# FFN pairs of a transformer layer: mixing the channels behind the third product, sums of x taken from PSUM, gates all 144 wide, weights in another order

## The chip, the cores and the metric

The kernel runs on one core of a Trainium2 chip. A core has TensorE (PE, whose weight loads are shown apart as PEld), VectorE (DVE), ScalarE (ACT), GpSimd (POOL) and SyncE (SP, which here only issues DMAs). All tensors of the computation are 32-bit floats. The metric is the device time of one execution in microseconds; lower is better.

## The reference

The layer takes x of 32 x 64 x 1024 and does two things in turn: a long convolution with attention on top, added to x, and then the FFN, added again. The change is in the FFN and in the weights and loads around its start:

```python
def _moe_lora(xf, gate_W, A, B):
    gate_probs = jax.nn.softmax(xf @ gate_W.T, axis=-1)
    weights, sel = jax.lax.top_k(gate_probs, TOP_K)          
    weights = weights / jnp.sum(weights, axis=-1, keepdims=True)
    w_dense = jnp.zeros((T, E), xf.dtype).at[jnp.arange(T)[:, None], sel].add(weights)
    h = jnp.einsum('td,erd->ter', xf, A)
    h = h * (w_dense[:, :, None] * SCALING)
    return jnp.einsum('ter,eor->to', h, B)
...
out = xf @ W_base.T + _moe_lora(xf, gate_W, A, B)
...
x = x + attention(convolution(x, ...), ...)
x = x + ffn(mix(x, weights, condition), ...)
```

`mix` multiplies the 64 positions of each of the 32 sequences by one of 16 matrices of 64 x 64, which the sequence's condition picks. What comes out is the FFN's input.

## The kernel before

The 2048 tokens are 16 tiles of 128, and two tiles are a pair: the FFN has `NP` = 8 pairs. Each engine runs its own program, written out by hand in order; semaphores with counts (`pe_p`, `v_xs`, `a_xfhi` and so on) tie them together.

A pair's product with W_base, 256 tokens x 1024 x 1024, is done as a Strassen-Winograd scheme: seven products (`product`, idx 0 to 6) of 128 x 512 x 512 instead of eight. Their left operands are four blocks of the mixed x (A11, A12, A22 and A21) and sums of them, S1 to S4. Each operand is kept as a high part in a format with a short mantissa and a low part that is the rest, and a product makes three passes (high by high, high by low, low by high), so it is 12 matmuls with 128x512 outputs. The right operands, combinations of W_base, are 14 units of weights (`w4_*`, two to a product). They are fetched by SP (`load_w4`), turned into a high part by ScalarE (`w4_hi`) and a low part by VectorE or, for units 7, 9, 11 and 13, by GpSimd (`w4_lo`).

For one pair PE does in order (`ffn_matmuls`): product 0, the gates and ranks (`gates_and_ranks`, 32 matmuls into PSUM bank 0), products 1, 2 and 3, two transposes of the weighted h (`turn_h`), product 4, six matmuls with the expert weights (`experts`), the channel mix of the next pair's two tiles (`mix_channels`, 128 small matmuls in the trace, into PSUM banks 0 to 3), product 5, two more expert matmuls, product 6. `added` makes PE wait until VectorE has taken a bank.

From the mixed x in PSUM, ScalarE copies the four blocks out (`x_hi`, into xs) and makes seven high parts from them (xf). VectorE forms the sums (`combine_x`) and the low parts of A11, A12 and A22 (`x_lo`), GpSimd the low parts of the sums (`combined_lo`). The gates of the next pair need the parts of A11, A12, S1 and A22. VectorE adds every finished bank into x1 (`add_to`), and picks the experts (`gate_choice`, `gate_weights_of_tokens`). SP stores x1 tiles when they are done and fetches those of the pair after next (`ffn_transfers`, `load_x1`, a ring of four tiles).

Ahead of pair 0, SP's queue (`attention_transfers`) holds, in order: x1 tiles 0 and 1, the gate weights, the store of x1 tile 14, a wait for the last projection but one, units 8 to 13 of the weights, the store of tile 15, the expert weights in two halves, x1 tiles 2 and 3. ScalarE's program for the FFN (`ffn_hi`) begins with a wait for the expert weights (`ld_p4`), VectorE's (`ffn_sums`) with the low part of weight unit 8.

## Time and profile before

| what | value |
|---|---|
| median of 3 runs | 909.04 us (907.42 to 910.8) |
| the profiled execution's own time | 911.1 us |
| its span, first to last instruction | 909.3 us |
| PE matmul busy | 876.0 us, 96% of the span |
| PE weight loads busy | 732.9 us, 81% |
| VectorE busy | 500.3 us, 55% |
| GpSimd busy | 465.9 us, 51% |
| ScalarE busy | 233.0 us, 26% |
| mean granted TensorE clock | 0.987 of full speed |

The busy share of PE is no measure of how near it is to its peak, since matmuls are pipelined and overlap in the records: what counts is the distance from one start to the next. All times of the profile are microseconds from the span's start. A granted clock of 1.00 is 2.4 GHz, 0.50 is 1.2 GHz. A row of the timeline merges neighbours of one kind: "x4" are four instructions, and the time is from the first's start to the last's end. What stands in square brackets is how long the engine was idle before the row, and who released it.

### The profile page before, as it was taken

How to read it: one execution, taken by the hardware profiler on the slowest of the kernel's cores; microseconds unless marked ns; L12 is line 12 of the kernel's file. 1: busy time of each engine (PE TensorE's matmuls, PEld its weight loads, DVE VectorE, ACT ScalarE, POOL GpSimd, SP SyncE). 2: the span in 40 equal slices, each digit the busy share in tenths (PEclk: the TensorE clock that was granted, in tenths of full speed). 3: DMA queues.
4: the chain of work that ended last, by engine and by line, in shares of the span. 5: the costliest groups of instructions: out<-in, count | busy, mean ns of one | idle time of the engine just before them, and what ended most of it. 6: DMA issues, size and time to landing. Idle time of an engine off the chain costs nothing.

```text
span 909.3 us, 24331 instructions
## 1 busy us (share of the span) xinstructions
PE 876.0 (96%) x10726; PEld 732.9 (81%) x10726; DVE 500.3 (55%) x880; ACT 233.0 (26%) x401; POOL 465.9 (51%) x346
## 2 busy tenths in 40 slices
PE   3999999999999999999999999999978999999998
PEld 3889999988888888887777777777766888888887
DVE  7465551123432222278887778888357666635663
ACT  4454542000000000032232223334233122211220
POOL 3444564103295557679878888877363233303330
PEclk9999999999999999999999999999998999988999
DMA  3789877315444322274444455553360221022201
GB/s 101 180 208 216 197 200 199 134 46 185 174 128 108 77 70 70 58 247 119 131 145 149 149 194 175 165 176 118 130 231 1 93 94 58 37 93 93 88 24 76
DMA packets 94554, 116.86 MB, mean 129 GB/s; under 512 B 44017, under 2 KB 58353, under 8 KB 94449
## 3 DMA queue, kind: packets, MB, share of 16 engines
q1 hardware_dynamic: 91456, 114.27, 42.3%
q8 instruction: 85, 1.39, 0.6%
q10 hardware_dynamic: 2480, 0.51, 0.3%
q0 software_dynamic: 512, 0.53, 0.2%
q14 instruction: 21, 0.16, 0.1%
HBM read 81.42 MB, written 33.85 MB: 127 GB/s over the span
## 4 chain that ended last, share of the span: by engine, by line
PE 83%; DVE 8%; DMA 2%; issue 2%; ACT 2%; SPq 1%; POOL 1%; DVEq 0%; POOLq 0%
PE ps L972 24%; PE ps L1250 19%; PE ps L1552 10%; PE ps L635 9%; PE ps L936 5%; PE ps L646 4%; PE ps L1206 3%; PE ps L1186 3%; DVE xf L1518 3%; PE ps L1568 2%; PE ps L1468 2%; ACT xs L1505 1%; PE ps L1570 1%; DMA toep<-kpad 1%; SPq L592 1%
## 5 line engine op out<-in xcount | busy, mean ns | idle before, releaser
L1552 PE MATMUL ps<-wb_hi,xf 128*128 128x512 f32 x448 | 153.3, 413 | 5.9 <-DVE x L1695 5.9
L1518 POOL TENSOR_TENSOR xf<-xs,xf 128x512 fp32r<-128x512 f32 x32 | 54.8, 1741 | 148.7 <-ACT xf L1511 148.7
L972 PE MATMUL ps<-y_hi,w_hi 128*128 128x512 f32 x320 | 125.3, 391 | 0.0
L972 PE MATMUL ps<-y_hi,w_lo 128*128 128x512 f32 x320 | 124.7, 390 | 0.0
L972 PE MATMUL ps<-y_lo,w_hi 128*128 128x512 f32 x320 | 124.7, 390 | 0.0
L1552 PEld LDWEIGHTS ps<-wb_hi,xf 128*128 128x128 f32 x448 | 88.5, 198 | 26.9 <-DVE x L1695 6.6
L1250 PE MATMUL ps<-y_hi 128*128 128x512 f32 x256 | 103.1, 403 | 0.2 <-issue 0.2
L635 PE MATMUL ps<-xc,toep 64*128 64x192 f32 (+4 forms) x1088 | 96.9, 330 | 3.5 <-DMA toep<-kpad 1.8
L1250 PE MATMUL ps<-y_hi,y_lo 128*128 128x512 f32 x256 | 100.2, 391 | 0.0
L1250 PE MATMUL ps<-y_lo,y_hi 128*128 128x512 f32 x256 | 100.2, 391 | 0.0
L635 PEld LDWEIGHTS ps<-xc,toep 64*128 64x128 f32 x1088 | 91.2, 187 | 6.6 <-issue 4.5
L1552 PE MATMUL ps<-wb_lo,xf 128*128 128x512 f32 x224 | 91.1, 406 | 0.0
L1084 POOL TENSOR_TENSOR rot<-rot,cst 128x512 f32<-128x512 f32 x40 | 53.7, 1343 | 58.1 <-DVE rot L1054 58.0
L1278 POOL TENSOR_TENSOR sc<-sc,stat 128x1024 f32<-128x1024 f32 x32 | 60.9, 1905 | 38.4 <-DVE stat L1274 38.4
L1054 DVE LOAD_MASK_SELECT rot<-ps x40 | 0.6, 14 | 134.1 <-PE ps L972 118.5
L972 PEld LDWEIGHTS ps<-y_hi,w_hi 128*128 128x128 f32 x320 | 60.1, 188 | 12.6
L972 PEld LDWEIGHTS ps<-y_hi,w_lo 128*128 128x128 f32 x320 | 60.1, 188 | 12.6
L972 PEld LDWEIGHTS ps<-y_lo,w_hi 128*128 128x128 f32 x320 | 60.1, 188 | 12.3
L1292 POOL TENSOR_TENSOR sc<-sc,stat 128x1024 f32<-128x1024 f32 x32 | 67.8, 2119 | 2.2 <-DVE stat L1288 2.2
L769 POOL TENSOR_TENSOR y_lo<-ym,y_hi 128x256 fp32r<-128x256 f32 x32 | 30.3, 948 | 70.2 <-ACT y_hi L758 70.0
L1088 POOL TENSOR_TENSOR rf<-rot,rc 128x512 f32<-128x512 f32 x40 | 52.8, 1320 | 17.8 <-DMA k_rows<-rf 14.8
L1695 DVE TENSOR_TENSOR x<-ps,x 128x512 f32<-128x512 f32 x64 | 42.1, 685 | 35.2 <-PE ps L1552 29.6
(183 smaller groups left out, 1596.4 us busy)
## 6 DMA issues: line engine op xcount, KB each, us to landing
toep<-kpad SPq DMA_DIRECT2D x124, 136.0 KB
xc<-in_dram SPq DMA_DIRECT2D x32, 256.0 KB, 4.5
q_rows<-rf SPq DMA_DIRECT2D x32, 256.0 KB, 2.6
q<-q_rows SPq DMA_DIRECT2D x16, 512.0 KB, 3.9
xr<-in_dram SPq DMA_DIRECT2D x16, 512.0 KB, 4.7
x_scratch<-xr SPq DMA_DIRECT2D x16, 512.0 KB, 3.0
x<-x_scratch SPq DMA_DIRECT2D x16, 512.0 KB, 4.3
out_dram<-x SPq DMA_DIRECT2D x15, 512.0 KB, 3.4
```

Of the source, the lines that this page charges most:

```text
L635: mm = pe.matmul(ps[:, 2 * (n % 3) + r, d * NB:NJ * NB], toep[rows, n % TR, at:at + P], xc[rows, n // XH % XR, 1 - c, n % XH, 0:(NJ - d) * ...
L646: mm = pe.matmul(ps[half * HALF:(half + 1) * HALF, 2 * (n % 3) + r, d * NB:NJ * NB], toep[rows, n % TR, at:at + HALF], xc[rows, n // XH % ...
L936: mm = pe.matmul(out, wv[a][:, j, h * P:(h + 1) * P], y[b][:, j, b0:b1, s0:s1], start=(j == 0 and a + b == 0), stop=(j == NJ - 1 and a == 1))
L972: mm = pe.matmul(kq_bank(n), w[a][:, j, :], yt[b][:, j, g * 512:(g + 1) * 512], start=(j == 0 and a + b == 0), stop=(j == NJ - 1 and a == 1))
L1084: gp.tensor_tensor(r, r, across(C("sin"), 8), ALU.mult).then_inc(g_rsin, 1)
L1088: gp.tensor_tensor(rf[:, (NVB + n) % SR, :], rot[:, n % RR, :], rc[:, n % RR, :], ALU.add).then_inc(g_rsum, 1)
L1250: mm = pe.matmul(ps[:, 6 + n, :], heads, wo(c, t)[:, n, :], start=(at == 0), stop=(at == 3 * NQT - 1))
L1278: gp.tensor_tensor(sc_groups(u), sc_groups(u), along(stat[:, u % CR, 0, :], S), ALU.subtract).then_inc(g_sub, 1)
L1292: gp.tensor_tensor(sc_groups(u), sc_groups(u), along(stat[:, u % CR, 2, :], S), ALU.mult).then_inc(g_prob, 1)
L1518: return eng.tensor_tensor(xf(i, op, 1)[:], xs(i, op), xf(i, op, 0)[:].bitcast(F32), ALU.subtract)
L1552: mm = pe.matmul(dst, xf(i, idx, a)[:, t, :], wb(c, idx, t), start=(start and t == 0 and a + c == 0), stop=(t == 3 and a == 1), skip_group ...
L1695: v.tensor_tensor(x, src, x, ALU.add).then_inc(v_sum_out, 1)
```

## The change

It is all in the FFN and the loads around its start.

- The channel mix of the next pair is moved from behind the expert matmuls to behind product 2, with a wait until VectorE has summed the gates' bank 0.
- The turned h goes to the sum bank that the pair doesn't use (bank 7 or 4), no longer to bank 1, into which the mix writes. The wait for the last projection's copy (`a_pr`) moves ahead of the first turn for that.
- ScalarE copies only A21 out of PSUM; the high parts of A22, A11 and A12 are made straight from PSUM (`x_of_mixed`), the high parts of the sums behind the turned h (`x_of_sums`): 8 operations a pair instead of 11.
- VectorE's sums and low parts take one operand from PSUM. They are seven as before, in two groups, `combine_first` ahead of the low part of h and `combine_last` behind it. `combined_lo` is `sums_lo` now, with the same four operations on GpSimd.
- The 16 gate matmuls of a pair whose left operand is a low part become 144 columns wide, as the other 16 are, instead of 72.
- SP fetches x1 tiles 2 and 3 before the weights, and units 12 and 13 behind the expert weights. ScalarE waits for the expert weights behind the gates' exponential of pair 0. VectorE takes the first add of pair 0 ahead of the low part of unit 8, and units 10, 12 and 13 change places with work on x.

```diff
 def attention_transfers(sp):
...
             sp.dma_start(wg_raw[:, :, 1, :], w_ffn[:, :, 0:NPROJ]).then_inc(ld_wg, 16)
+            load_x1(sp, 2)
             store_x1(sp, NPAIR - 2)
+            load_x1(sp, 3)
             sp.wait_ge(pe_y, 2 * NPAIR - 1)
-            for u in range(8, 14):
+            for u in range(8, 12):
                 load_w4(sp, u)
             store_x1(sp, NPAIR - 1)
...
-            load_x1(sp, 2)
-            load_x1(sp, 3)
+            load_w4(sp, 12)
+            load_w4(sp, 13)
...
+        def mixed_lo(v, i, op):
+            hi_made(v, i, op)
+            v.tensor_tensor(by_batch(xf(i, op, 1)[:]), mixed(*MIXED[op]), by_batch(xf(i, op, 0)[:]).bitcast(F32),
+                            ALU.subtract).then_inc(v_xflo, 1)
...
+        def combine_first(v, i):
+
+            hi_made(v, i, A22)
+            v.wait_ge(a_x21, i + 1)
+            v.tensor_tensor(by_batch(xs(i, S1)), mixed(1, 1), by_batch(xs(i, S3)), ALU.add).then_inc(v_xs, 1)
+            mixed_lo(v, i, A22)
+            hi_made(v, i, A12)
+            v.wait_ge(v_xs, 4 * i + 1)
+            v.tensor_tensor(by_batch(xs(i, S3)), mixed(0, 0), by_batch(xs(i, S3)), ALU.subtract).then_inc(v_xs, 1)
+            v.tensor_tensor(by_batch(xs(i, S2)), by_batch(xs(i, S1)), mixed(0, 0), ALU.subtract).then_inc(v_xs, 1)
+
+        def combine_last(v, i):
+            v.wait_ge(v_xs, 4 * i + 3)
+            v.tensor_tensor(by_batch(xs(i, S4)), mixed(0, 1), by_batch(xs(i, S2)), ALU.subtract).then_inc(v_xs, 1)
+            mixed_lo(v, i, A11)
+            mixed_lo(v, i, A12)
...
 def gates_and_ranks(pe, i):
...
-                        pe.matmul(gate_bank[:, k, :], xf(i, op, 0)[:, t, :], w[:, first + t, :, :].rearrange("p a n -> p (a n)"),
-                                  start=(op in (A11, S1) and t == 0), stop=False)
-                        mm = pe.matmul(gate_bank[:, k, 0:NPROJ], xf(i, op, 1)[:, t, :], w[:, first + t, 0, :],
-                                       start=False, stop=(op in (A12, A22) and t == 3))
+                        for part in range(2):
+                            mm = pe.matmul(gate_bank[:, k, :], xf(i, op, part)[:, t, :], w[:, first + t, :, :].rearrange("p a n -> p (a n)"),
+                                           start=(op in (A11, S1) and t + part == 0), stop=(op in (A12, A22) and t + part == 4))
...
 def ffn_matmuls(pe):
...
                 product(pe, i, 2, sum_bank(i))
+                if i + 1 < NP:
+                    pe.wait_ge(v_gate, GATE_STEPS * i + 1)
+                    mix_channels(pe, 2 * i + 2)
+                    mix_channels(pe, 2 * i + 3)
                 added(pe, 8 * i + 2)
                 product(pe, i, 3, D_BANK)
+                if i == 0:
+                    pe.wait_ge(a_pr, 2 * NPAIR)
                 turn_h(pe, i)
...
 def ffn_hi(act):
-            act.wait_ge(ld_p4, 16 * 2)
...
                 if i == 0:
+                    act.wait_ge(ld_p4, 16 * 2)
                     act.activation(bexp_hi[:], bexp_raw[:], ACT.Copy).then_inc(a_p4, 1)
-                    for u in range(10, 14):
-                        w4_hi(act, u)
+                    w4_hi(act, 10)
+                    w4_hi(act, 11)
+                if i + 1 < NP:
+                    x_of_mixed(act, i + 1)
                 act.wait_ge(pe_ht, i + 1)
...
 def ffn_sums(v):
-            w4_lo(v, 8)
             for i in range(NP):
                 v.wait_ge(pe_p, 7 * i + 1)
                 add_to(v, i, 0, 0, sum_bank(i))
+                if i == 0:
+                    w4_lo(v, 8)
                 gate_choice(v, i)
```

How the programs of the engines stand before and after, at three places. PE in pair 0, around the mix of tiles 2 and 3 (x1_2, x1_3; wb_hi_9 is the high part of weight unit 9, xf_0_4_1 the low part of operand 4), before:

```order
L1552 MATMUL ps<-wb_hi_9,xf_0_4_1 128x512
L1584 MATMUL ps<-bexp_hi,ht 128x512
L1585 MATMUL ps<-bexp_lo,ht 128x512
L1584 MATMUL ps<-bexp_hi,ht 128x512
L1585 MATMUL ps<-bexp_lo,ht 128x512
L1584 MATMUL ps<-bexp_hi,ht 128x512
L1585 MATMUL ps<-bexp_lo,ht 128x512
L1468 MATMUL ps<-craw,x1_2 64x64 x32
L1468 MATMUL ps<-craw,x1_3 64x64 x32
L1552 MATMUL ps<-wb_hi_10,xf_0_5_0 128x512
```

And after, the same mix of the same pair:

```order
L1561 MATMUL ps<-wb_hi_5,xf_0_2_0 128x512
L1561 MATMUL ps<-wb_lo_5,xf_0_2_0 128x512
L1561 MATMUL ps<-wb_hi_5,xf_0_2_1 128x512
L1471 MATMUL ps<-craw,x1_2 64x64 x32
L1471 MATMUL ps<-craw,x1_3 64x64 x32
L1561 MATMUL ps<-wb_hi_6,xf_0_3_0 128x512
```

The mix stood between the expert matmuls and product 5 (unit 10), and stands between products 2 (unit 5) and 3 (unit 6).

VectorE in pair 0, from the last part of the gate steps (hw is the weighted h, ht its low part), before:

```order
L1688 TENSOR_TENSOR hw<-gsum,gt 128x2x64 x2
L1695 TENSOR_TENSOR x1_0<-ps,x1_0 128x512
L1412 TENSOR_TENSOR wb_lo_10<-wb_raw_10,wb_hi_10 128x1024
L1412 TENSOR_TENSOR wb_lo_12<-wb_raw_12,wb_hi_12 128x1024
L1717 TENSOR_TENSOR ht<-ps,ht 64x256
L1695 TENSOR_TENSOR x1_1<-ps,x1_1 128x512 x2
L1488 TENSOR_TENSOR xs_1_1<-xs_1_6,xs_1_4 128x512
L1491 TENSOR_TENSOR xs_1_4<-xs_1_0,xs_1_4 128x512
```

After:

```order
L1705 TENSOR_TENSOR hw<-gsum,gt 128x2x64 x2
L1712 TENSOR_TENSOR x1_0<-ps,x1_0 128x512
L1415 TENSOR_TENSOR wb_lo_10<-wb_raw_10,wb_hi_10 128x1024
L1520 TENSOR_TENSOR xs_1_1<-ps,xs_1_4 128x2x4x64
L1511 TENSOR_TENSOR xf_1_6_1<-ps,xf_1_6_0 128x2x4x64
L1524 TENSOR_TENSOR xs_1_4<-ps,xs_1_4 128x2x4x64
L1525 TENSOR_TENSOR xs_1_2<-xs_1_1,ps 128x2x4x64
L1736 TENSOR_TENSOR ht<-ps,ht 64x256
L1415 TENSOR_TENSOR wb_lo_12<-wb_raw_12,wb_hi_12 128x1024
L1529 TENSOR_TENSOR xs_1_3<-ps,xs_1_2 128x2x4x64
```

Four operations on the next pair's x stand ahead of the low part of h now, and read PSUM.

SP's queue ahead of the FFN, before:

```order
L1137 DMA x1_scratch<-xr_2 128x1024
L1402 DMA wb_raw_8<-ffn_t_rows 128x1024
L1402 DMA wb_raw_9<-ffn_t_rows 128x1024
L1402 DMA wb_raw_10<-in_10_dram 128x2x512
L1402 DMA wb_raw_11<-in_10_dram 128x2x512
L1402 DMA wb_raw_12<-ffn_t_rows 128x1024
L1402 DMA wb_raw_13<-ffn_t_rows 128x1024
L1137 DMA x1_scratch<-xr_0 128x1024
L1170 DMA bexp_raw<-in_11_dram 64x1024 x2
L1383 DMA x1_2<-x1_scratch 128x1024
L1383 DMA x1_3<-x1_scratch 128x1024
```

After:

```order
L1386 DMA x1_2<-x1_scratch 128x1024
L1137 DMA x1_scratch<-xr_2 128x1024
L1386 DMA x1_3<-x1_scratch 128x1024
L1405 DMA wb_raw_8<-ffn_t_rows 128x1024
L1405 DMA wb_raw_9<-ffn_t_rows 128x1024
L1405 DMA wb_raw_10<-in_10_dram 128x2x512
L1405 DMA wb_raw_11<-in_10_dram 128x2x512
L1137 DMA x1_scratch<-xr_0 128x1024
L1172 DMA bexp_raw<-in_11_dram 64x1024 x2
L1405 DMA wb_raw_12<-ffn_t_rows 128x1024
L1405 DMA wb_raw_13<-ffn_t_rows 128x1024
```

The loads of x1 tiles 2 and 3 went up, those of units 12 and 13 down.

## Rows read from the trace of the kernel before

**Rows 1.** Chain that ended last, FFN: start, length, engine, line, count

```profile
726.93 2.07 PE ps L1468 x128
...
738.39 0.30 PE ps L1568
742.12 8.29 PE ps L1552 x36
...
794.01 0.30 PE ps L1568
...
856.05 0.31 PE ps L1568
...
883.83 0.31 PE ps L1568
```

**Rows 2.** Timeline, PE, from product 0 to the gates of pair 2

```profile
737.48 0.39 PE L1552 MATMUL ps<-wb_hi,xf 128*128 128x512 f32 x1
738.39 0.30 PE L1568 MATMUL ps<-wg,xf 128*128 128x144 f32 x1 [0.52 <-DVE xf L1518]
738.53 0.24 PE L1570 MATMUL ps<-wg,xf 128*128 128x72 f32 x1
738.60 0.31 PE L1568 MATMUL ps<-wg,xf 128*128 128x144 f32 x1
```

**Rows 3.** Timeline, PE weight loads, first of these gates and first behind them

```profile
738.36 0.19 PEld L1568 LDWEIGHTS ps<-wg,xf 128*128 128x128 f32 x1 [0.91 <-issue]
...
741.92 0.19 PEld L1552 LDWEIGHTS ps<-wb_hi,xf 128*128 128x128 f32 x1
```

**Rows 4.** Timeline, PE, matmuls 256 columns wide, earlier in the kernel

```profile
165.01 0.28 PE L936 MATMUL ps<-y_hi,w_lo 128*128 128x256 f32 x1
165.13 0.28 PE L936 MATMUL ps<-y_hi,w_hi 128*128 128x256 f32 x1
```

**Rows 5.** Stretches: us, busy PE, PEld, DVE, ACT, POOL, PEclk, DMA share, GB/s

```profile
681.00:687.00 6.00, 5.44 (x13) 4.30 (x14) 5.48 (x17) 3.81 (x5) 4.70 (x3) 0.50 0.02 8
687.00:688.00 1.00, 1.00 (x5) 0.80 (x4) 1.00 (x1) 1.00 (x2) 1.00 (x1) 0.69 0.00 0
695.00:698.00 3.00, 3.00 (x8) 2.32 (x8) 1.20 (x3) 0.00 (x0) 0.00 (x0) 0.52 0.00 0
797.00:803.00 6.00, 6.00 (x19) 5.04 (x19) 1.93 (x12) 0.22 (x1) 0.00 (x0) 0.50 0.76 266
```

**Rows 6.** Timeline, ACT, POOL and DVE, between the mix and the gates

```profile
729.03 2.07 ACT L1505 ACTIVATE xs<-ps 128x512 f32<-128x512 f32 x4 [5.78 <-PE ps L1468]
732.42 6.85 POOL L1518 TENSOR_TENSOR xf<-xs,xf 128x512 fp32r<-128x512 f32 x4 [20.93 <-ACT xf L1511]
733.07 5.07 DVE L1518 TENSOR_TENSOR xf<-xs,xf 128x512 fp32r<-128x512 f32 x3
738.06 2.47 DVE L1695 TENSOR_TENSOR x<-ps,x 128x512 f32<-128x512 f32 x4
```

**Rows 7.** Timeline, SP's queue, loads of x1 in pair 2

```profile
743.01 1.54 SPq L1383 DMA_DIRECT2D x<-x_scratch  x2
```

**Rows 8.** Page, DMA issues: count, KB each, median us to landing

```profile
x<-x_scratch SPq DMA_DIRECT2D x16, 512.0 KB, 4.3
```

**Rows 9.** Timeline, PE, its two long waits in pair 0

```profile
681.56 0.80 PE L1552 MATMUL ps<-wb_hi,xf 128*128 128x512 f32 x1 [5.75 <-DVE x L1695]
...
692.55 0.44 PE L1579 MATMUL ps<-cst,hw 128*128 128x128 f32 x2 [2.44 <-DVE hw L1688]
```

**Rows 10.** Timeline, POOL, ACT and DVE, what pair 0 waits for

```profile
671.74 1.27 POOL L1330 TENSOR_TENSOR xr<-pr,xr 128x512 f32<-128x512 f32 x1
678.60 2.00 ACT L1408 ACTIVATE wb_hi<-wb_raw 128x1024 fp32r<-128x1024 f32 x2 [9.45 <-DMA bexp_raw<-in_dram]
679.68 1.23 DVE L1412 TENSOR_TENSOR wb_lo<-wb_raw,wb_hi 128x1024 fp32r<-128x1024 f32 x1 [10.12 <-ACT wb_hi L1408]
686.97 2.26 DVE L1678 TENSOR_TENSOR ge<-cst,gt 128x32 f32<-128x32 f32 x1
```

More of the change, by code:

```diff
@@ L297, in build @@
         v_wd, a_wg, v_wg = [signal(n) for n in ("v_wd", "a_wg", "v_wg")]
-        pe_mix, a_xraw, v_xs, a_xfhi, v_xflo, g_xflo = [signal(n) for n in (
-            "pe_mix", "a_xraw", "v_xs", "a_xfhi", "v_xflo", "g_xflo")]
+        pe_mix, a_x21, v_xs, a_xfhi, v_xflo, g_xflo = [signal(n) for n in (
+            "pe_mix", "a_x21", "v_xs", "a_xfhi", "v_xflo", "g_xflo")]
         pe_g, v_gate, a_gate, v_h, pe_ht, a_hthi, v_htlo = [signal(n) for n in (
@@ L1320, in attention_softmax @@
                 if w == NUNIT:
-                    combine_x(v, 0)
-                    x_lo(v, 0)
+                    combine_first(v, 0)
+                    combine_last(v, 0)
             gate_weights(v)
@@ L1368, in attention_hi @@
                 if w == NUNIT:
-                    x_hi(act, 0)
+                    x_of_mixed(act, 0)
+                    x_of_sums(act, 0)
             gate_weights_hi(act)
@@ L1503, in x_hi @@
                 act.wait_ge(g_p4, 1)
-            for op, k, half in ((S3, 1, 0), (A22, 1, 1), (A11, 0, 0), (A12, 0, 1)):
-                act.activation(by_batch(xs(i, op)), mixed(k, half), ACT.Copy).then_inc(a_xraw, 1)
-            for op in BUILD:
-                if op in COMBINED:
-                    act.wait_ge(v_xs, 4 * i + COMBINED[op])
-                else:
-                    act.wait_ge(a_xraw, 4 * i + 4)
+            act.activation(by_batch(xs(i, S3)), mixed(1, 0), ACT.Copy).then_inc(a_x21, 1)
@@ L1511, in x_hi, with x_of_sums @@
+            for op in TURNED:
+                act.activation(by_batch(xf(i, op, 0)[:]), mixed(*MIXED[op]), ACT.Copy).then_inc(a_xfhi, 1)
+        def x_of_sums(act, i):
+            for op in LO_GP:
+                act.wait_ge(v_xs, 4 * i + COMBINED[op])
                 act.activation(xf(i, op, 0)[:], xs(i, op), ACT.Copy).then_inc(a_xfhi, 1)
         def hi_made(eng, i, op):
-            eng.wait_ge(a_xfhi, NOP * i + BUILD.index(op) + 1)
-        def lo(eng, i, op):
-            hi_made(eng, i, op)
-            return eng.tensor_tensor(xf(i, op, 1)[:], xs(i, op), xf(i, op, 0)[:].bitcast(F32), ALU.subtract)
@@ L1520, in x_lo @@
-        def x_lo(v, i):
-            v.wait_ge(v_xs, 4 * i + 4)
-            for op in (A11, A12, A22):
-                lo(v, i, op).then_inc(v_xflo, 1)
-        def combined_lo(gp, i):
+            eng.wait_ge(a_xfhi, NOP * i + (TURNED + LO_GP).index(op) + 1)
+        def mixed_lo(v, i, op):
+            hi_made(v, i, op)
+            v.tensor_tensor(by_batch(xf(i, op, 1)[:]), mixed(*MIXED[op]), by_batch(xf(i, op, 0)[:]).bitcast(F32),
+                            ALU.subtract).then_inc(v_xflo, 1)
@@ L1714, in ffn_sums @@
                     w4_lo(v, 10)
+                if i + 1 < NP:
+                    combine_first(v, i + 1)
+                v.wait_ge(a_hthi, i + 1)
+                v.tensor_tensor(ht[NH:, :, :].rearrange("p k n -> p (k n)"), turned_h(i)[NH:, :],
+                                ht[NH:, :, :].rearrange("p k n -> p (k n)").bitcast(F32), ALU.subtract).then_inc(v_htlo, 1)
+                if i == 0:
                     w4_lo(v, 12)
-                v.wait_ge(a_hthi, i + 1)
-                v.tensor_tensor(ht[NH:, :, :].rearrange("p k n -> p (k n)"), turned_h[NH:, :],
-                                ht[NH:, :, :].rearrange("p k n -> p (k n)").bitcast(F32), ALU.subtract).then_inc(v_htlo, 1)
+                if i + 1 < NP:
+                    combine_last(v, i + 1)
                 v.wait_ge(pe_p, 7 * i + 5)
```

49 lines of the change are left out of this document (20 added, 29 removed).

## The prediction

> **What bounds the kernel now.** I read the page first: PE is busy 96% of the span, and 83% of the chain that ended last is PE. So the FFN part is read as a string of PE work, and I look for three things: where PE waits, where its granted clock is low, and what it does in between. The chain that ended last gives the beat [rows 1]. The gate matmuls of pairs 2, 4, 6 and 7 begin at 738.39, 794.01, 856.05 and 883.83. Pairs 2 to 4 take 27.81 us each, pairs 4 to 6 take 31.02 us each, pair 6 takes 27.78 us. So there is an ordinary beat of 27.8 us, and two pairs that cost 3.2 us more (6.4 in all).
>
> The ordinary beat is nearly solid PE work: 84 matmuls of the products at 0.23 us each (36 took 8.29) [rows 1], gates of 3.56 us, eight expert matmuls (1.8), two transposes (0.2) and the channel mix (2.07) [rows 1]. What is left is one hole: the last matmul of product 0 starts at 737.48, its successor could start 0.23 later, and the first gate matmul starts at 738.39, released by VectorE's low parts of x [rows 2]. That is 0.68 us, and each of the seven changes from one pair to the next has the same. Behind it stands a chain: mix ends at 729.0, ScalarE copies four blocks out of PSUM in 2.07, VectorE forms sums and then three low parts in 5.07, which end at 738.14 [rows 6]. Those three would take 0.6 to 0.7 us each; they take 1.7 each because they alternate with GpSimd's four (6.85). The four adds at 738.06, which read one operand from PSUM, keep 0.62 us each while GpSimd is still running until 739.27 [rows 6].
>
> The two long pairs are explained by the clock: from 797 to 803, in pair 4, it stood at 0.50, the 1.2 GHz level [rows 5], and a stretch alike lies in pair 5, from 828 to 834. Both began inside gates that followed a hole, and PE waited for nothing in them. Lastly pair 0: PE stands 5.75 us before 681.56 and 2.44 us before 692.55 [rows 9], and works at the low level from 681.56 to some 687.6 and for 3.4 us up to 698 [rows 5].
>
> **The change, part by part.** All of it is laid against the profiled execution: span 909.3, its own time 911.1; the median of the three runs is 909.0, so 2 us lower.
>
> *Channel mix behind product 2, the x blocks built earlier.* The matmuls are the same in number and kind, the mix with 128 of 0.016 us; nothing is added on PE but a wait for the gate sums, which VectorE forms 0.3 us behind the gates, 5 us earlier. From the start of product 0 (time 0): gates 2.7 to 6.3, product 1 to 9.0, product 2 to 11.8, mix to 13.9, product 3 to 16.6, turn, product 4 to 19.6, experts 21.0, product 5 to 23.7, product 6 to 26.9. ScalarE's copies run 14.1 to 16.2 [rows 6], VectorE's first four to 18.0, the low part of h to 18.5 (PE wants it at 19.6), the last three to 20.4, GpSimd's four from 18.2 to at most 25. All of x is ready before 26.9, and the first gate wants it at 29.6. So the hole goes: 0.68 in each of the 6 beats from pair 1 to 7, **-4.1 us**. What is late next is the low part of h, with 1.1 us to spare. ScalarE's turned h now stands behind four copies, but these end 0.8 before it. VectorE's seven operations all read one operand from PSUM now, so by the adds of [rows 6] they take 0.6 to 0.7 and don't alternate with GpSimd.
>
> The Trainium skill has a rule against this: VectorE: DVE Perf Modes, section The TRN2 errata, gives VectorE 58 fixed cycles from SBUF and 120 from PSUM. As an estimate by that page this is 0.065 us more for each operation, 0.45 us for seven, and its rules for authors say to copy out of PSUM first when there are many operations. By it the spare 1.1 us would be 0.8 and the sum would be the same but for some 0.3 in pair 0; the adds in the trace show nothing of it (0.62 apart).
>
> *Clock.* Both low stretches follow a hole that goes, and the gates behind it now stream 32 times 144 columns in the same time instead of 16 times 144 and 16 times 72. The gates of the other pairs came through at full clock with the same hole, so it was a near thing; with less idleness on both counts I take both stretches as gone: **-6.4 us**. If neither goes: 0. If the mix in its new place brings new ones, each costs 3.2; the mix stood beside product work before as well, without one.
>
> *Gates all 144 wide.* 16 of 32 matmuls of each pair grow by 72 columns. The loads of weights start evenly, from 738.36 to 741.92 in 32 steps, 0.111 us each, whatever the width [rows 3]. The matmul starts alternate by 0.15 and 0.07 [rows 2], but two of them make two loads, so the load sets the pace. The nearest row for a wide one is a 128x256 matmul with the same load: they follow at 0.12 [rows 4]. Bounds: 0 if the load paces; 32 x 0.009 x 8 = +2.3 us if 144 columns cost what 256 do; 32 x 0.037 x 8 = +9.5 us if the 0.148 behind each 144-wide one is its own time. I take **0**; a gain is excluded, as the loads stay.
>
> *Pair 0: weights reordered.* Before, the weight units 8 and 9 are converted on ScalarE behind a wait for the expert weights; those are fetched behind the last store of x1, which waits for GpSimd's add at 671.74 to 673.0 [rows 10]. ScalarE so stands 9.45 us until 678.60, VectorE 10.12 until 679.68 with its first add queued behind the weight unit, and PE with product 2 behind that add [rows 9, 10]. After, the add goes first (about 670), units 8 and 9 wait only for themselves, and the wait for the expert weights stands behind the gates' exponential. The 5.75 goes. With it goes the 2.44 before the turn, which came of VectorE's gate steps starting late and meeting GpSimd's units (2.26 for one of 32 columns [rows 10]). The low clock behind the two holes goes too: 6.1/2 + 3.4/2 = 4.7. With the 0.68 at the gates of pair 1 this is 13.6 us. Given back: the gate steps of pair 0 now meet GpSimd's expert weights (some 677 to 680) and one more unit of some 2.5 (twice the 1.27 of 512 columns [rows 10]), and VectorE must do unit 10 (1.2), the four of combine_first (2.6) and the low part of h before the experts: I get about 687.5 against PE's 686.2, and 0.9 us again for the sum behind unit 12. Units 12 and 13 are fetched behind the expert weights now: at some 672.5 instead of ahead of them, landed 5 us later, needed by product 6 at 692: hidden. I take 2 us given back (0 to 6): **-11.6 us**.
>
> Moved loads: x1 tiles 2 and 3 are fetched earlier on SP; the second waits for store 14 to land, and what is queued behind it, the weight units, waits for a later projection matmul anyway. Hidden; if not, product 3 and not product 0 is the first to miss a unit. Turned h in the idle sum bank costs nothing but a wait for a bank long free.
>
> Sum: -4.1 - 6.4 - 0 - 11.6 = **-22.1 us**: span 887.2, its execution 889.0, against the median 886.9. I say **887**.
>
> **The rivals.**
>
> (a) The clock falls all the same. For it: pairs alike (2, 3, 6) held the clock and 4 and 5 didn't, so something besides the hole decides. Against it: all four low stretches of the FFN begin at or right behind a hole of PE. Two stretches left: 887 + 6.4 = 893.4.
>
> (b) Pair 0's waits move instead of going. VectorE has the gate steps, three weight units and seven operations for x between 676 and 691, against GpSimd's units. With 5 us more and one low stretch on it: about 892 to 895.
>
> (c) 144-wide matmuls at 0.148: +9.5, so 896.5. For it: the recorded 0.30 of a 144-wide is longer than the 0.28 of a 256-wide [rows 2, 4]. Against it: the even loads.
>
> (d) Slower than before: the mix now wants the next x1 tiles 11.8 us into a pair, not 22. Before, these were issued from 743.01 to 744.5 (pair 2 begins at 735.0) [rows 7] and take 4.3 to land [rows 8], so 13.8 into the pair: 2 us too late. It decides at whether the stores move forward: they wait for the pair's last adds, at 738.06 to 740.5 [rows 6], because these stand behind the low parts of x. Behind the change nothing stands ahead of them, the last add ends 1 us into the next pair, the loads land at 8 to 10, and there is a spare of 2 to 4. If they don't move, six pairs wait 2 us each before the mix and the clock falls in each: 887 + 12 + 7 x 3.2 = 921.
>
> (e) The hole at the gates stays, as GpSimd's part is late: then +4.1 and the 6.4: 897.5. Its parts would have to slip by 5 us.
>
> **How the numbers follow.** The forecast 0.60 (885 to 890). (a) 0.14, (b) 0.12, (c) 0.05, (d) 0.04, (e) 0.01, and 0.04 for less than 884, if pair 0 gives nothing back. The range from 883.5 to 893.5 takes in the forecast, (a) and half of (b): some 0.82. About 0.5% (4.5 us) is what a measurement of this kernel can tell from no change. All but (d) lie below 904.5: faster 0.94, slower 0.04, within 0.02.
>
> **What would show it.** Gate starts from pair 1 to 7 should be 27.1 us apart, all of them, with no idle row ahead of the gates; the clock should be 1.00 from 669 on. Gates should last 3.56 us per pair. PE's idle before product 2 should be gone, and the longest one in pair 0 should stand before the experts, 1 to 2 us, released by VectorE's low part of h. Gates of pair 1 should begin near 699. It is wrong if a wait for an x1 load stands before a mix, if load starts in the gates spread beyond 0.12, or if a stretch at 1.2 GHz is left behind 700.

## The result, and the profile after

The changed kernel takes 886.24 us (median of 4 runs, 885.33 to 889.1), the kernel before beside it 909.55 us (4 runs, 907.42 to 910.8). The ratio is 0.9751, interval 0.9722 to 0.9781: 2.5% less, about 23 us. A second set of runs, beside experiments 8 and 9, gave 887.43 us against 910.35, ratio 0.9758 [0.9731, 0.9785].

| | before | after |
|---|---|---|
| span of the profiled execution | 909.3 | 884.4 |
| first product of pair 0 begins | 666.59 | 665.78 |
| from there to the gates of pair 1 | 44.01 | 31.56 |
| beats from pair 1 to pair 7 (six) | 27.78, 27.79, 27.83, 31.02, 31.02, 27.78 | 26.95 each |
| first product to the end of the span ("FFN" below) | 242.71 | 218.64 |
| start of the last matmul of product 0 to the first gate matmul, pairs 1 to 7 | 0.86 to 0.91 | 0.23 |

"FFN" is the measure used for all runs, since what lies ahead of the first product is the same work in all of them and still ends between 663.7 and 668.9, whatever the kernel. The FFN became 24.1 us shorter; the other 0.8 of the span's 24.9 lies ahead of it and isn't the change's.

The chain that ended last, of the kernel after (start, length, engine, line, count; what [rows 1] was before; the gates are line 1578 now, the products 1561, the mix 1471):

```profile
697.50 3.53 PE ps L1578 x32
...
706.52 2.02 PE ps L1471 x128
...
724.44 3.53 PE ps L1578 x32
...
859.18 3.53 PE ps L1578 x32
```

The chain counts a piece 0.16 later than the timeline does; its steps are the same. From 697.50 to 859.18 are six beats, 161.68 us, none longer than another. The timeline of PE at the gates of pair 2, which answers to [rows 2]:

```profile
723.83 0.39 PE L1561 MATMUL ps<-wb_lo,xf 128*128 128x512 f32 x1
724.05 0.39 PE L1561 MATMUL ps<-wb_hi,xf 128*128 128x512 f32 x1
724.28 0.68 PE L1578 MATMUL ps<-wg,xf 128*128 128x144 f32 x5
```

The first gate matmul follows the last of product 0 by 0.23, with no bracket: the hole is gone. And the row of one long stretch (length, busy PE, PEld, DVE, ACT, POOL, then PEclk), where [rows 5] had 0.50 to 0.69:

```profile
669.00:885.00 216.00, 210.83 (x1889) 178.18 (x1888) 113.73 (x292) 39.59 (x77) 48.23 (x34) 1.00 0.23 79
```

The clock is at its 2.4 GHz level through the whole FFN. Beside the mix the other engines now stand like this (timeline, ACT, DVE and POOL, pair 1; [rows 6] was the same work before):

```profile
708.62 0.60 ACT L1497 ACTIVATE xs<-ps 128x512 f32<-128x512 f32 x1 [6.43 <-PE ps L1471]
709.11 1.57 ACT L1499 ACTIVATE xf<-ps 128x512 fp32r<-128x512 f32 x3
...
711.54 0.68 DVE L1525 TENSOR_TENSOR xs<-xs,ps 128x512 f32<-128x512 f32 x1
712.25 0.43 DVE L1736 TENSOR_TENSOR ht<-ps,ht 64x256 fp32r<-64x256 f32 x1
712.71 0.69 DVE L1529 TENSOR_TENSOR xs<-ps,xs 128x512 f32<-128x512 f32 x1
713.32 1.28 DVE L1511 TENSOR_TENSOR xf<-ps,xf 128x512 fp32r<-128x512 f32 x2
...
712.80 5.04 POOL L1537 TENSOR_TENSOR xf<-xs,xf 128x512 fp32r<-128x512 f32 x4 [19.15 <-ACT xf L1504]
```

VectorE's low parts take 0.6 each from start to start where they took 1.7, though GpSimd runs beside them, and GpSimd's four take 5.04 instead of 6.85. What is left of waits in the FFN are two in pair 0 (timeline, PE), where [rows 9] had 5.75 and 2.44:

```profile
686.67 0.47 PE L1594 MATMUL ps<-bexp_hi,ht 128*128 128x512 f32 x1 [1.04 <-DVE ht L1736]
...
691.31 0.50 PE L1594 MATMUL ps<-bexp_hi,ht 128*128 128x512 f32 x1 [0.31 <-DVE x L1712]
```

From start to start these are gaps of 1.42 and 0.69 us, so 1.2 and 0.5 more than the pace of 0.23.

### The profile page after: what moved, and what is told of

It is laid out like the page before. It is cut to its first block, busy times and chain, and to the rows that moved or that the text cites. A ratio compares the mean times of both kernels' runs of the same rounds, so it can differ in the third digit from the quotient of the medians.

```text
span 884.4 us, 24307 instructions
## 1 busy us (share of the span) xinstructions
PE 862.1 (97%) x10726; PEld 724.9 (82%) x10726; DVE 475.6 (54%) x880; ACT 220.8 (25%) x377; POOL 454.7 (51%) x346
## 4 chain that ended last, share of the span: by engine, by line
PE 93%; DVE 3%; DMA 2%; SPq 1%; issue 1%; ACT 0%
PE ps L972 25%; PE ps L1252 20%; PE ps L1561 16%; PE ps L635 9%; PE ps L936 5%; PE ps L646 4%; PE ps L1578 3%; PE ps L1208 3%; PE ps L1188 3%; PE ps L1471 2%; DMA toep<-kpad 1%; SPq L592 1%; PE ps L1594 1%; PE ps L1595 1%; DMA kpad<-ksb 1%
## 5 line engine op out<-in xcount | busy, mean ns | idle before, releaser
L1561 PE MATMUL ps<-wb_hi,xf 128*128 128x512 f32 x448 | 146.4, 394 | 0.0
L1537 POOL TENSOR_TENSOR xf<-xs,xf 128x512 fp32r<-128x512 f32 x32 | 42.1, 1347 | 132.4 <-ACT xf L1504 128.6
L1561 PEld LDWEIGHTS ps<-wb_hi,xf 128*128 128x128 f32 x448 | 84.1, 188 | 17.4
L1561 PE MATMUL ps<-wb_lo,xf 128*128 128x512 f32 x224 | 87.3, 390 | 0.0
```

The costliest lines, as they stand in the source:

```text
L1537: gp.tensor_tensor(xf(i, op, 1)[:], xs(i, op), xf(i, op, 0)[:].bitcast(F32), ALU.subtract).then_inc(g_xflo, 1)
L1561: mm = pe.matmul(dst, xf(i, idx, a)[:, t, :], wb(c, idx, t), start=(start and t == 0 and a + c == 0), stop=(t == 3 and a == 1), skip_group ...
```

## The experiments

The theory to test had four parts: the six holes went because x is mixed earlier and taken from PSUM; the clock held because the holes went; the 144-wide gates cost nothing; pair 0 shrank because ScalarE no longer waits for the expert weights first. Each kernel below is either the changed one with a part undone (1, 4, 5, 9) or altered further (6, 7), or the one before with parts added (2, 3, 8, 10). All ratios are to the kernel before on the same chip. Gaps are from one matmul's start to the next one's. The edits shown are shortened, and `...` stands for what is left out. FFN, beats and gaps are those of one profiled execution of each kernel; the medians are over 4 to 7 executions. Each execution's mean granted clock is on record too, so (1 - mean) x 2 x span is an estimate of the time that it spent at 1.2 GHz: 23.6 us for the mean of 0.987 of the kernel before, whose trace shows four stretches of 23.9 in all.

### 1. Low-part gate matmuls 72 wide again

In the changed kernel:

```diff
-    mm = pe.matmul(gate_bank[:, k, :], xf(i, op, 1)[:, t, :], w[:, first + t, :, :]...)
+    mm = pe.matmul(gate_bank[:, k, 0:NPROJ], xf(i, op, 1)[:, t, :], w[:, first + t, 0, :]...)
```

> The changed kernel with the 16 gate matmuls on low parts back at 72 columns; all else as changed. Theory (the hole ahead of the gates is what let the clock fall): no hole, so the clock stays at 1.00 whatever the width, the gates take 3.5 to 3.6 us per pair and the time is that of the changed kernel, 886 within 1.5. Rival (the width holds the clock): stretches at 0.50 come back in two or more pairs, 3.2 us each, 892 to 900.

Measured: 887.86 us, ratio 0.9755 [0.9716, 0.9794]; beat 26.98, gates 3.49 us, clock 1.00 everywhere, FFN 218.94. Once the holes are gone the width is worth nothing measurable in either direction: the gates are 0.04 us shorter, the beat 0.03 longer.

### 2. The kernel before, all gate matmuls 144 wide, nothing else

```diff
+    for part in range(2):
+        mm = pe.matmul(gate_bank[:, k, :], xf(i, op, part)[:, t, :], w[:, first + t, :, :]...)
```

> The kernel before with nothing but the 16 gate matmuls on low parts widened from 72 to 144 columns. It still has the 0.68 us hole ahead of the gates in seven pairs. Theory (the hole lets the clock fall): the two stretches in pairs 4 and 5, or as many elsewhere, stay, 909 within 2. Rival (the width holds the clock): pairs 1 to 6 all take 27.8 us, no stretch at 0.50 behind pair 0, 902 to 903. If 144-wide matmuls cost time of their own: gates longer than 3.56 us per pair, up to 4.7, and 911 to 918.

Measured: 904.44 us, ratio 0.993 [0.9903, 0.9957]; FFN 236.62, 6.1 less than before. All six beats are 27.77. The hole is there (timeline, PE), and yet the long stretches with it keep the clock:

```profile
735.14 0.39 PE L1552 MATMUL ps<-wb_hi,xf 128*128 128x512 f32 x1
736.03 0.64 PE L1569 MATMUL ps<-wg,xf 128*128 128x144 f32 x4 [0.50 <-DVE xf L1518]
...
736.00:875.00 139.00, 136.45 (x1271) 113.86 (x1272) 83.72 (x186) 32.13 (x65) 34.41 (x21) 1.00 0.22 77
```

So the holes alone did not bring the clock down: with the same holes and wide gates it held in all of them. Six of the seven executions have a mean clock of 0.994, 10.8 us at 1.2 GHz by the estimate, and the two stretches in pair 0 of this trace are 10.2; the seventh has 0.992, so some 4 us more.

### 3. The kernel before, with the weights' order alone

The loads, ScalarE's wait and VectorE's weight units as in the change; mix, sources and widths as before.

```diff
 def ffn_hi(act):
-    act.wait_ge(ld_p4, 16 * 2)
...
+        act.wait_ge(ld_p4, 16 * 2)
         act.activation(bexp_hi[:], bexp_raw[:], ACT.Copy).then_inc(a_p4, 1)
```

> The kernel before with the weights part alone: x1 tiles 2 and 3 fetched early, units 12 and 13 fetched and converted late, ScalarE's wait for the expert weights behind the gates' exponential, the first add of pair 0 ahead of unit 8. Mix, operands of the sums and gate widths as before. Theory (pair 0 is a matter of this order alone): PE's 5.75 and 2.44 us waits and both low stretches in pair 0 go, gates of pair 1 begin at 698 to 700 instead of 710.6, the beats stay at 27.8 with their holes, 897 within 3. Rival (it needs the mix's new place too, since VectorE is the one in pair 0): 901 or more.

Measured: 895.09 us, ratio 0.9818 [0.9778, 0.9858]; FFN 229.96. Pair 0 shrinks by all that it shrinks in the full change: the gates of pair 1 begin 31.29 us after the first product (31.56 in the full change). The holes of 0.9 stay, and there are again two long beats of 31.0, but in pairs 1 and 2 and no longer in 4 and 5 (rows of stretches below). The profiled execution is the slowest of the five, 899.33 us with a mean clock of 0.992; the others have 0.992 to 0.998, so the clock fell in all of them, but in three for 4 to 7 us and not for 14. That is why the median fell by 15.7 us and this FFN by 12.75.

```profile
702.00:708.00 6.00, 6.00 (x18) 4.94 (x19) 1.93 (x12) 0.22 (x1) 0.00 (x0) 0.50 0.75 259
733.00:739.00 6.00, 6.00 (x19) 5.03 (x19) 1.93 (x12) 0.22 (x1) 0.00 (x0) 0.50 0.72 257
760.00:766.00 6.00, 5.49 (x41) 4.91 (x40) 3.99 (x10) 0.22 (x1) 1.74 (x2) 1.00 0.45 178
```

### 4. The changed kernel, with ScalarE's old wait

ScalarE waits for the expert weights first again, and VectorE takes the low part of unit 8 ahead of its first add.

```diff
 def ffn_hi(act):
+    act.wait_ge(ld_p4, 16 * 2)
...
 def ffn_sums(v):
+    w4_lo(v, 8)
```

> The changed kernel with two lines of the weights part undone: ScalarE waits for the expert weights ahead of units 8 and 9, and VectorE makes unit 8's low part ahead of the first add. SP's queue as changed. Theory: PE waits again before product 2 of pair 0, some 4 us, until the expert weights are in (676) and ScalarE's and VectorE's unit and the add are through (679), a low stretch may follow, beats of 26.95 behind it: 890 to 895. Rival (the store and SP's order did it): no wait over 1 us, 886 to 888.

Measured: 893.79 us, ratio 0.981 [0.9769, 0.9852]; FFN 225.67, 7.0 more than the full change, all of it in pair 0. ScalarE and PE show the old picture of [rows 9, 10] (timeline, ACT and PE, then the stretch behind):

```profile
676.82 2.00 ACT L1411 ACTIVATE wb_hi<-wb_raw 128x1024 fp32r<-128x1024 f32 x2 [9.42 <-DMA bexp_raw<-in_dram]
...
679.79 0.79 PE L1561 MATMUL ps<-wb_hi,xf 128*128 128x512 f32 x1 [4.00 <-DVE x L1712]
...
679.00:685.00 6.00, 5.21 (x12) 3.80 (x12) 5.51 (x17) 3.05 (x4) 4.69 (x3) 0.50 0.00 0
```

### 5. The changed kernel, with x taken from SBUF

The mix keeps its new place; ScalarE copies all four blocks out as before, and VectorE reads both operands from SBUF.

```diff
 def mixed_lo(v, i, op):
-    v.tensor_tensor(by_batch(xf(i, op, 1)[:]), mixed(*MIXED[op]), by_batch(xf(i, op, 0)[:]).bitcast(F32), ...)
+    v.tensor_tensor(xf(i, op, 1)[:], xs(i, op), xf(i, op, 0)[:].bitcast(F32), ...)
```

> The changed kernel with x taken through SBUF again, in the new place: ScalarE copies all four blocks out of PSUM and makes seven high parts (11 operations), VectorE's sums and low parts read SBUF only and meet GpSimd's. Theory (the mix's new place alone closes the hole, PSUM as a source only shortens a chain that has room): beats stay at 26.95, clock 1.00, some 1 to 2 us more in pair 0, 887 to 889. Rival (the PSUM sources are needed): PE waits for the low part of h before the experts in every pair, 0.5 us or more each, 890 and above. By the rule of the Trainium skill, VectorE: DVE Perf Modes, section The TRN2 errata, operations on SBUF would be 0.065 us shorter than on PSUM; the rows will show.

Measured: 902.88 us, ratio 0.9919 [0.9889, 0.9949]; FFN 235.15, 16.5 more than the full change. The theory on record was missed, and its rival, 890 and above, held in the time but not in the place of the wait. Two things change along with the sources: ScalarE has 11 operations a pair for 8, and the low part of A22 stands in the last group on VectorE and not in the first. No hole stands ahead of the gates, but the beat is 28.3, longer than before the change, with a new wait of PE ahead of the last two expert matmuls (timeline, PE, DVE and POOL, pair 1):

```profile
727.65 0.50 PE L1598 MATMUL ps<-bexp_hi,ht 128*128 128x512 f32 x1 [1.08 <-DVE x L1716]
...
721.81 5.06 DVE L1514 TENSOR_TENSOR xf<-xs,xf 128x512 fp32r<-128x512 f32 x3
726.90 2.68 DVE L1716 TENSOR_TENSOR x<-ps,x 128x512 f32<-128x512 f32 x4
...
721.18 6.82 POOL L1541 TENSOR_TENSOR xf<-xs,xf 128x512 fp32r<-128x512 f32 x4 [23.81 <-ACT xf L1507]
```

The three low parts alternate with GpSimd's four again, 1.7 us each. Now the add behind product 4 is queued behind them; it begins at 726.90, and PE needs its bank free at 726.4. So with x from SBUF the new place costs 0.5 us a pair against the old kernel's ordinary beat of 27.8. The six beats are half of the 16.5 (170.00 against 161.68). The other 8.2 are in pair 0, where the same wait is longer and a stretch of 6.8 us at 1.2 GHz goes with it (timeline, PE):

```profile
697.02 0.79 PE L1598 MATMUL ps<-bexp_hi,ht 128*128 128x512 f32 x1 [4.90 <-DVE x L1716]
```

### 6. All gate matmuls 72 wide

This kernel leaves out the products with the low parts of the gate and rank weights, so it serves to measure and is not a version to use.

```diff
-    mm = pe.matmul(gate_bank[:, k, :], xf(i, op, part)[:, t, :], w[:, first + t, :, :]...)
+    mm = pe.matmul(gate_bank[:, k, 0:NPROJ], xf(i, op, part)[:, t, :], w[:, first + t, 0, :]...)
```

> The changed kernel with all 32 gate matmuls of a pair 72 columns wide; the products with the low parts of the gate and rank weights are left out. No hole ahead of the gates. If the weight loads set the pace, the gates stay at 3.4 to 3.55 us per pair for half the columns. Theory (no fall of the clock without a hole): clock 1.00, 886. Rival (few enough columns let it fall without a hole): stretches at 0.50 in some or all pairs, 3.2 us each, up to 910.

Measured: 890.16 us, ratio 0.9783 [0.9752, 0.9814]; gates 3.49 us, as in experiment 1, so 32 matmuls of half the columns take what 144-wide ones take (3.53), within 0.04. The beats are 26.98 and the clock 1.00 up to pair 6. But in pair 7 the clock falls, behind gates that follow product 0 with no hole (timeline, PE, and the stretch below). It is no single case: the mean clocks of the four executions are 0.998, 0.998, 0.996 and 0.994, an estimated 3.5 to 10.7 us at 1.2 GHz, where the changed kernel has 1.00 in nine of its ten and 0.999 in the other.

```profile
857.83 0.39 PE L1561 MATMUL ps<-wb_hi,xf 128*128 128x512 f32 x1
858.05 1.20 PE L1578 MATMUL ps<-wg,xf 128*128 128x72 f32 x10
...
861.00:865.00 4.00, 4.00 (x15) 3.38 (x15) 1.93 (x12) 0.22 (x1) 0.00 (x0) 0.57 0.00 0
```

### 7. Another order of VectorE in pair 0

To see whether VectorE's order is all that is left in pair 0: the low part of h ahead of the first combination, and the add behind product 4 ahead of unit 12 and the last combination. The diff shows the first of these two moves; the second is made in the same way.

```diff
-    if i + 1 < NP:
+    if 0 < i and i + 1 < NP:
         combine_first(v, i + 1)
     v.wait_ge(a_hthi, i + 1)
     v.tensor_tensor(ht[NH:, ...], turned_h(i)[NH:, :], ...)
+    if i == 0:
+        combine_first(v, i + 1)
```

> The changed kernel with VectorE's order changed in pair 0 alone: the low part of h ahead of combine_first, and the add behind product 4 ahead of the low part of unit 12 and combine_last. Theory (both waits left in pair 0 are VectorE's order): the 1.2 us before the experts and the 0.5 us before the last two expert matmuls go, gates of pair 1 come 29.9 us behind product 0's start instead of 31.6, 1.7 us less, 884.5. Rival (the low part of unit 12 or of x is late instead): product 6 or product 0 of pair 1 waits as long, 886.

Measured: 885.45 us, ratio 0.9727 [0.9702, 0.9752]; FFN 216.75. It was run once more beside the changed kernel itself:

> The changed kernel itself, again, as the measure for the next run. Both theories: 885 to 888 us, FFN (first product to the end of the span) 218.6, gates of pair 1 31.6 us behind the first product, two gaps of the product stream of over 0.5 us (1.4 ahead of pair 0's experts, 0.7 ahead of its last experts), beat 26.95.

> The changed kernel with VectorE's order in pair 0 altered: the low part of h ahead of the first combination, the add behind product 4 ahead of the last combination. Theory (what is left in pair 0 is VectorE's order alone): gates of pair 1 29.7 behind the first product, no gap over 0.5 us, 1.9 us less than the changed kernel on the same chip. Rival (the waits only move into pair 1): pair 1's beat grows by as much, no difference.

Measured: the changed kernel 887.43 us (FFN 218.68), this one 885.06 us, ratio 0.9728 [0.9703, 0.9754], FFN 216.75 again. The gates of pair 1 begin 29.67 us after the first product both times, 1.9 earlier, and no gap over 0.5 is left in the FFN. The traces agree to 0.05; the two ratios' intervals overlap, so by the times alone the gain would not be shown.

### 8. The kernel before, with the weights' order and wide gates

Experiments 2 and 3 together; mix and sources as before, so the diff is the sum of theirs.

> The kernel before with two parts of the change: the weights' order and sources of pair 0, and all gate matmuls 144 wide; the mix stays behind the experts, sources of x stay in SBUF. Theory (the clock falls only where the hole ahead of the gates meets narrow gate matmuls): granted clock 1.00 from pair 1 on, holes of 0.9 us between starts stay, beats 27.77, gates of pair 1 31.3 behind the first product, FFN 223.3, 889 to 891 us. Rival (the hole alone can bring the clock down, only where is chance): one or two beats of 31.0, 893 to 897 us.

Measured: 890.97 us, ratio 0.9787 [0.9759, 0.9816]; FFN 223.26; beats 27.80 once and 27.77 five times; gates of pair 1 31.18 after the first product. All seven holes are there, none costs the clock, and the mean clock is 1.00 in all four executions (timeline, PE, and a stretch of one beat):

```profile
725.89 0.39 PE L1554 MATMUL ps<-wb_hi,xf 128*128 128x512 f32 x1
726.75 0.75 PE L1571 MATMUL ps<-wg,xf 128*128 128x144 f32 x5 [0.48 <-DVE xf L1520]
...
838.00:866.00 28.00, 27.52 (x258) 22.98 (x258) 16.93 (x39) 6.42 (x13) 7.08 (x5) 1.00 0.21 76
```

### 9. The changed kernel, with the mix in its old place

```diff
     product(pe, i, 2, sum_bank(i))
-    if i + 1 < NP:
-        pe.wait_ge(v_gate, GATE_STEPS * i + 1)
-        mix_channels(pe, 2 * i + 2)
-        mix_channels(pe, 2 * i + 3)
...
     experts(pe, 1, 1, other_bank(i), start=True).then_inc(pe_x, 1)
+    if i + 1 < NP:
+        mix_channels(pe, 2 * i + 2)
+        mix_channels(pe, 2 * i + 3)
```

`x_of_mixed`, `combine_first` and `combine_last` go back with it, behind the turned h and the adds. Sources stay in PSUM.

> The changed kernel with the channel mix put back to its old place, behind the experts' matmuls and just ahead of the gates' turn; sources of x stay in PSUM, gates 144 wide. Theory (the new place is needed): the turned operands come late for the gates, a hole of 0.5 to 0.9 us stands ahead of them in each pair, beat 27.5 to 27.8, 890 to 893 us. Rival (x taken from PSUM alone closes the hole: from the mix's end to the gates' operands some 5.7 us, with 5.9 of product 0 to hide them): beat 26.95, 885 to 888 us.

Measured: 887.49 us, ratio 0.974 [0.9707, 0.9773]; FFN 220.46. All six beats are 26.95. My theory that the new place was needed fell. VectorE's last low parts stand at 722.58 and take 1.28, GpSimd's four begin at 722.02 and take 5.06 (the gates use the first), and the first gate matmul comes at 726.95, 0.23 behind its forerunner (timeline, DVE, POOL and PE):

```profile
722.58 1.28 DVE L1511 TENSOR_TENSOR xf<-ps,xf 128x512 fp32r<-128x512 f32 x2
...
722.02 5.06 POOL L1537 TENSOR_TENSOR xf<-xs,xf 128x512 fp32r<-128x512 f32 x4 [21.89 <-DVE xs L1525]
...
726.73 0.39 PE L1561 MATMUL ps<-wb_hi,xf 128*128 128x512 f32 x1
726.95 0.79 PE L1578 MATMUL ps<-wg,xf 128*128 128x144 f32 x6
```

In this trace the place is worth 1.8 us of FFN, all in pair 0: with no mix between product 2 and the turn, PE stands waiting there for the weighted h (timeline, PE, with the stretch behind it, then DVE and POOL):

```profile
682.82 0.41 PE L1589 MATMUL ps<-cst,hw 128*128 128x128 f32 x2 [1.58 <-DVE hw L1703]
...
683.00:687.00 4.00, 3.90 (x11) 2.89 (x10) 3.06 (x4) 2.27 (x3) 1.38 (x1) 0.57 0.00 0
...
677.89 4.78 DVE L1703 TENSOR_TENSOR hw<-gsum,gt 128x128 f32<-128x128 f32 x2
...
677.74 2.41 POOL L1656 TENSOR_TENSOR bexp_lo<-bexp_raw,bexp_hi 128x1024 fp32r<-128x1024 f32 x1 [3.13 <-ACT bexp_hi L1641]
680.12 2.41 POOL L1415 TENSOR_TENSOR wb_lo<-wb_raw,wb_hi 128x1024 fp32r<-128x1024 f32 x1
```

That gap is 1.97 from start to start, and 3.4 us at 1.2 GHz follow it, which cost 1.7 of the 1.8. The changed kernel has the same slow `hw` (4.88 us, last section), but the mix stands in front of the wait. The run times don't show the gain: two of the four executions have a mean clock of 0.998 like this one and two have 1.00, and the median, 887.49, is that of the changed kernel on the same chip, 887.43.

The missing mix is not the whole reason for the gap either. Experiment 8 has no mix there and no such wait, since `hw` ran 1.8 us ahead of GpSimd's operation on the expert weights (timeline, DVE and POOL):

```profile
679.98 0.49 DVE L1692 TENSOR_TENSOR hw<-gsum,gt 128x128 f32<-128x128 f32 x2
...
681.76 2.42 POOL L1645 TENSOR_TENSOR bexp_lo<-bexp_raw,bexp_hi 128x1024 fp32r<-128x1024 f32 x1 [4.20 <-ACT bexp_hi L1631]
```

Experiments 8, 9 and 5 and the changed kernel share the weights' order and the wide gates, so their FFN shows what the other two parts do there: neither 223.3 (8), sources alone 220.5 (9), place alone 235.2 (5), both 218.6.

### 10. The kernel before, with x taken from PSUM alone

Mix in its old place, weights in their old order, low gates 72 wide: only the sources of x (and the idle bank for the turned h).

```diff
 def mixed_lo(v, i, op):
+    v.tensor_tensor(by_batch(xf(i, op, 1)[:]), mixed(*MIXED[op]), by_batch(xf(i, op, 0)[:]).bitcast(F32), ...)
```

> The kernel before with one part of the change alone: blocks and sums of x taken from PSUM (and the turned h in the idle sum bank); the mix stays behind the experts, the weights in their old order, the low-part gate matmuls 72 wide. Theory (the sources alone close the hole, and without the hole narrow gates keep the clock): beat 26.98 in all six, granted clock 1.00 from pair 1 on, 43 to 44 us from the first product to the gates of pair 1 as before, FFN 231 to 232, 897 to 899 us. Rival (narrow gates lose the clock now and then without a hole, as once with all gates 72 wide): one or two beats of some 30, 901 to 904 us. Second rival (the low gates' hole needs the earlier mix when the gates are narrow): holes of 0.9 between starts, 902 to 909 us.

Measured: 896.53 us, ratio 0.9865 [0.9839, 0.9891]; FFN 229.48; all six beats 26.98, clock 1.00 behind pair 0 (timeline, DVE and PE; stretch):

```profile
731.35 1.28 DVE L1509 TENSOR_TENSOR xf<-ps,xf 128x512 fp32r<-128x512 f32 x2
...
735.49 0.39 PE L1559 MATMUL ps<-wb_hi,xf 128*128 128x512 f32 x1
735.72 0.23 PE L1575 MATMUL ps<-wg,xf 128*128 128x144 f32 x1
735.78 0.24 PE L1577 MATMUL ps<-wg,xf 128*128 128x72 f32 x1
...
724.00:870.00 146.00, 146.00 (x1439) 123.67 (x1438) 74.33 (x197) 29.21 (x58) 29.60 (x24) 1.00 0.21 75
```

Five executions have a mean clock of 0.996 and one 0.994, so none was at 1.2 GHz longer than the 10.2 us that this trace has in pair 0, within the rounding; the 43 of the kernel before on four chips have 0.985 to 0.992, an estimated 14 to 27 us.

ScalarE's shorter list (8 operations for 11) is a rival to the sources as such, and the traces leave little to it. VectorE's first sum starts 1.2 us behind the end of the mix in both kernels (728.22 here, 730.14 before). From there to the end of the last low part it takes 4.4 us here and 8.0 before, and 3.2 of these 3.6 lie in the three low parts.

One part of the change, alone, closes all holes and keeps the clock: 13.2 us of the FFN's 24.1, of which 11.4 are in the beats behind pair 1's gates (173.23 to 161.88) and 1.8 in pair 0.

## Why the prediction was right, point by point

**The total.** 887.0 was forecast, 886.24 measured, the span 887.2 against 884.4 (0.8 of that lies ahead of the FFN). The profiled execution saved 24.1 us in the FFN where the sum had 22.1. That the forecast is off by less than 1 all the same is luck in part: the sum gave 889.0 for an execution like the profiled one, which took 886.22, and 2.1 of these 2.8 were made up by the step from the profiled execution before (911.1) to its median (909.0). After the change the two are the same.

**The holes, -4.1.** Size right: 0.90 to 0.23 between starts, six times 0.67, is 4.0. The beats gave 1.1 more than holes and clock together, since the beat is 26.95 and not 27.1: 0.03 in the gates and some 0.1 in several spots of the product stream, none over 0.1. These come with the sources as well: experiment 9, with the mix in its old place, has 26.95, and experiment 8, with x from SBUF, has 27.77, of which hole and gates explain all but 0.1. Why the product stream is that much shorter stays open.
The reason was half wrong. The step that failed is the one that let the hole go because the mix stands behind product 2 and all of x is "ready before 26.9". The timetable held (in pair 1 the low part of h ended 1.6 us before PE wanted it; 1.1 was forecast), but it was not what closed the hole. The four combinations settle it, by gap ahead of the gates and beat:

| | x from SBUF | x from PSUM |
|---|---|---|
| mix behind the experts | gap 0.86 to 0.91, beat 27.8 (before, 8) | gap 0.23, beat 26.95 to 26.98 (9, 10) |
| mix behind product 2 | gap 0.23, beat 28.3 (5) | gap 0.23, beat 26.95 (after) |

The prediction had the needed rows and their meaning: the low parts take 1.7 because they alternate with GpSimd, and ops with one operand in PSUM don't. It didn't carry them through: three low parts at 0.6 instead of 1.7 save 3.2 us against a hole of 0.68. That sum alone says that the sources suffice.

**The rule on PSUM sources.** The operations with an operand in PSUM follow at 0.60 to 0.61 and the adds at 0.6, as in [rows 6]. Two sums of the kernel before that read SBUF alone, with GpSimd at rest, follow at 0.61 as well (730.94 and 731.55), so nothing of 0.065 us more shows, and the sources are one of the two large gains, not a cost. What did matter is something else that the Trainium skill states. On the rows first: VectorE operations with two SBUF inputs ran 1.7 apart beside GpSimd (experiment 5), those with one ran 0.6 apart (after), GpSimd's own went from 6.82 to 5.04, and in pair 0 a small `hw` operation waited out two operations of GpSimd (experiment 9). The Trainium skill, SBUF — State Buffer, section Who interferes with whom, says that "A DVE instruction with two SBUF inputs contends with a GpSimd instruction that reads SBUF" and that one with a single SBUF input doesn't; these traces agree with both halves.

**The clock, -6.4.** Size right (two beats of 31.02 gone, 6.46). The reason named, less idleness "on both counts", was right as far as it went, and the runs separate the counts (pairs 1 to 7 of each profiled execution; the numbers in brackets are the experiments):

| gates | hole of 0.9 ahead of them | no hole |
|---|---|---|
| half 144, half 72 wide | fell in 2 of 7 pairs (before), 2 of 7 (3) | in none of 7 (1), none of 7 (10) |
| all 144 wide | in none of 7 (2), none of 7 (8) | in none of 7, in each of after, 4, 5, 7 and 9 |
| all 72 wide | not tried | in 1 of 7 (6) |

Either remedy suffices. So wide gates are worth 6 us on the kernel before and nothing on the one after, and the change pays for the same 6.4 twice. Which pair falls stays open: it went from 4 and 5 to 1 and 2 when only pair 0 changed its length. These are counts from one profiled execution per kernel. The mean clocks of the other executions bear them out, though a mean doesn't say where a stretch lay. All 43 executions of the kernel before lost more than the 10.2 us of pair 0, and all five of experiment 3 lost some though its trace has no stretch in pair 0. The executions of the changed kernel and of 1, 7 and 8 have 0.999 or 1.00; those of 10, and six of the seven of 2, lost no more than pair 0's part. The four of 6 all lost some, so the one fall in its trace is no exception. The run times fit too (experiment 2 gained 6 us in its FFN and the same in its median, 910.83 to 904.44).

**Gates all 144 wide, 0.** Right. Gates last 3.53 with 144 columns, 3.49 with 72, 3.56 before with a mixture behind a hole: the loads of the operands pace them. Rival (c), 0.148 for a wide one, fell, and (e) with the holes.

**Pair 0, -11.6.** Measured -12.45; the weights' order alone gave -12.7 (experiment 3) and putting the old wait back cost 7.0 (experiment 4). The given-back part was forecast as 2 (0.9 of it at the last experts) and was 1.7, in the two places named and by the engines named: 1.2 ahead of the experts, released by VectorE's low part of h, and 0.5 ahead of the last ones, by the add behind unit 12. Mis-sized was the low clock: 4.7 taken, but the stretches of 6.8 and 3.4 us are worth half of 10.2, 5.1. What I had charged as costs of VectorE's place in line, experiment 7 recovers whole, 1.9 us, by order alone. Rival (b), waits that move, did not happen.
The parts don't add up: sources -13.2, weights -12.75, width -6.1 make -32.1 alone and -24.1 together. Of the 8.0 between them 6.5 is the clock, which sources and width both bring. The rest lies in pair 0: the sources alone take 1.8 us off it, but put on top of weights and width (8 to 9) they add 2.2, for the collision of `hw` with GpSimd and the clock behind it. So what the sources still give in that order is 2.8 us of FFN, and 3.5 by the medians (890.97 to 887.49).

**Rival (d), late x1 tiles.** Its deciding point held: the stores moved forward. The two loads are issued 1.3 us into the pair (timeline, SP):

```profile
695.53 0.34 SPq L1448 DMA_DIRECT2D out_dram<-x  x1
695.92 2.84 SPq L1386 DMA_DIRECT2D x<-x_scratch  x2
```

The page gives 4.4 us to landing, so about 703 for the second, and the mix begins at 706.45: 3 us to spare, in the 2 to 4 forecast.
